# A graph layer whose issuing queue loads x before xn, and whose ScalarE takes the first norms before the tail of the previous step

## The reference, cut to what matters

```python
xn = layernorm(x)
# gnn: neighbour sum, then two linear layers
support = (1 + eps) * xn + segment_sum(edge_weight[:, None] * xn[src], dst, 12500)
gnn = relu(support @ W1.T + b1) @ W2.T + b2
# mix: 1x1 convolutions (only the centre taps meet data), hyperbolic maps, per-node linear attention
h = relu(batchnorm(conv(logmap0(proj(xn)), w_qkv)))
t = logmap0(proj(proj(expmap0(h)))); s = grouped_conv(t, w_dw, w_pw)
q, k, v = split(logmap0(proj(expmap0(concat(t, s)))))
out = attention(relu(q), relu(k), v) / (sum(v) + 1e-15)
mix = proj(expmap0(conv(logmap0(proj(expmap0(out))), w_res) + b_res))
x2 = x + gnn + mix
# ffn: one top-k over all nodes (k = 6249) picks the rows that get the FFN
x3 = layernorm(x2); w = x3 @ wr + br
y = gelu(x3 @ w1 + b1) @ w2 + b2       # kept only for the selected nodes, scaled by w
return x2 + x3 + scatter(y * w, top_k(w))
```

## Time and profile before

| | |
|---|---|
| median of 3 runs | 2587.64 us (2585.16 to 2588.34) |
| profiled execution | 2587.11 us, span of its instructions 2584.8 us |
| mean granted TensorE clock | 0.981 |
| busy share: PE, PEld, DVE, ACT, POOL | 93%, 69%, 67%, 55%, 64% |
| instructions | 44369 |

### The profile page before, as it was taken

One profiled execution on the slowest core, in us unless ns is written; L12 is line 12 of the kernel. 1 busy time (PEld: TensorE's weight loads), 2 busy tenths in 40 slices (PEclk: granted clock), 3 DMA queues, 4 the chain that ended last, 5 costly groups with the idle time before them and its releaser, 6 DMA issues.

```text
span 2584.8 us, 44369 instructions
## 1 busy us (share of the span) xinstructions
PE 2406.0 (93%) x13536; PEld 1795.6 (69%) x13536; DVE 1740.2 (67%) x5895; ACT 1431.4 (55%) x3219; POOL 1662.4 (64%) x1834
## 2 busy tenths in 40 slices
PE   4688999999999999999999999999899999999896
PEld 4665677776777776777776677777677777666686
DVE  7857576576665767657667676676766766767557
ACT  3545565565655656556555565565655656556431
POOL 1236777677776777777767777676776776777500
PEclk9889999999999999999999999999999999999998
DMA  6733444434444344443443444434444343344338
GB/s 208 252 103 103 131 116 116 117 114 131 115 118 116 113 117 123 122 121 114 116 117 114 131 115 116 118 112 125 115 122 119 114 124 110 114 132 116 88 118 283
DMA packets 225215, 327.42 MB, mean 127 GB/s; under 512 B 80845, under 2 KB 168510, under 8 KB 224956
## 3 DMA queue, kind: packets, MB, share of 16 engines
q0 software_dynamic: 84656, 231.94, 30.9%
q1 hardware_dynamic: 140300, 92.36, 12.1%
HBM read 285.70 MB, written 38.45 MB: 125 GB/s over the span
## 4 chain that ended last, share of the span: by engine, by line
PE 57%; DVE 37%; DMA 3%; issue 2%; ACT 1%; POOL 0%; SPq 0%; DVEq 0%
PE qkv L1451 14%; PE bank L1463 13%; PE bank L1356 11%; DVE rings L1155 6%; PE bank L1416 3%; PE bank L1425 3%; PE bank L1400 3%; DVE bank L1175 3%; DVE work L1180 3%; DVE work L1169 3%; DVE bank L1174 2%; PE qkv L1380 2%; DVE bank L1168 2%; DVE bank L1179 2%; DVE work L1178 2%
## 5 line engine op out<-in xcount | busy, mean ns | idle before, releaser
L958 POOL DMA_INDIRECT rings<-xn_dram,window x1715 | 1634.6, 953 | 694.3 <-issue 398.4
L1356 PE MATMUL bank<-rings 128*64 128x256 f32 x4410 | 662.7, 393 | 10.1 <-DMA rings<-xn_dram,window 7.1
L1155 DVE TENSOR_SCALAR rings<-iota,window_dst,window 128x64 f32<-128x64 f32 (+1 forms) x1715 | 490.1, 341 | 216.6 <-PE bank L1356 205.6
L1356 PEld LDWEIGHTS bank<-rings 128*64 128x64 f32 x4410 | 319.1, 137 | 276.2 <-issue 105.5
L1451 PE MATMUL qkv<-work,ffn_weights 128*128 128x256 f32 x1568 | 369.7, 384 | 0.0
L1463 PE MATMUL bank<-ffn_weights,work 128*128 128x256 f32 x1568 | 359.5, 382 | 0.0
L1463 PEld LDWEIGHTS bank<-ffn_weights,work 128*128 128x128 f32 x1568 | 293.8, 190 | 54.0 <-issue 16.2
L1048 ACT ACTIVATE work<-qkv,fb 128x256 f32<-128x256 f32 x392 | 160.1, 473 | 305.0 <-PE qkv L1451 304.5
L1451 PEld LDWEIGHTS qkv<-work,ffn_weights 128*128 128x128 f32 x1568 | 292.1, 191 | 52.5 <-ACT work L1048 16.2
L1370 PE MATMUL bank<-resident,weights 128*128 128x256 f32 x1176 | 285.6, 386 | 0.3
L1370 PEld LDWEIGHTS bank<-resident,weights 128*128 128x128 f32 x1176 | 217.7, 192 | 45.3 <-ACT work L1061 19.2
(11 more groups left out here) (261 smaller groups left out, 3267.2 us busy)
## 6 DMA issues: line engine op xcount, KB each, us to landing
rings<-xn_dram,window POOLq DMA_INDIRECT x1715
xn_dram<-work SPq DMA_DIRECT2D x14, 896.0 KB, 7.9
work<-xn_dram SPq DMA_DIRECT2D x49, 256.0 KB, 3.0
work<-in_x SPq DMA_DIRECT2D x48, 256.0 KB
out<-work SPq DMA_DIRECT2D x48, 256.0 KB
work<-in_x SPq DMA_DIRECT2D x7, 896.0 KB, 5.9
rings<-in_x SPq DMA_DIRECT2D x6, 896.0 KB, 10.0
rings<-out SPq DMA_DIRECT2D x6, 896.0 KB, 9.1
```

Source lines behind the costliest of these rows:

```text
L958: nc.gpsimd.indirect_dma_start(out=msg[G_ % RING][:, :], out_offset=None, in_=xn_dram[:, :], in_offset=bass.IndirectOffsetOnAxis(ap=window ...
L1155: v.tensor_scalar(one_hot(i, k, 0, len(quarters)), iota[:, quarters[0] * H:(quarters[-1] + 1) * H], window_dst[b][:, k:k + 1], window[b][: ...
L1356: te.matmul(agg[h][side * H:(side + 1) * H], one_hot(i, k, REACHES[k].index(q), 1), msg[gathered % RING], start=first, stop=n == STEP_PROD ...
```

## The change

Two orders are edited; no instruction is added or taken out. On SP, x of pair i - 1 is loaded before xn of pair i. On ACT, `mix_norms(i, 0)` and `mix_s_seed(i, 0)` move to the head of the step, ahead of `mix_n4_seed(j)`, `tail_supT(j)`, `ffn_x3T(m)` and `mix_exp(j)`; `tail_g1(j)` stays behind those.

```diff
@@ main_sync
             for i in range(1, NS):
+                load_x(sp, i - 1)
                 load_xn(sp, i)
-                load_x(sp, i - 1)
                 if i + 1 < NS:
                     load_window(sp, i + 1)
                 store_rows(sp, i - 1)
@@ main_scalar, step(i, j, m)
                 last = i == NS - 1
+                mix_norms(i, 0)
+                mix_s_seed(i, 0, mix)
                 if j >= 0:
                     mix_n4_seed(j, tail)
                     tail_supT(j)
                     if m is not None:
                         ffn_x3T(m)
                     mix_exp(j)
-                mix_norms(i, 0)
-                mix_s_seed(i, 0, mix)
-                if j >= 0:
                     tail_g1(j)
                 mix_v(i, 0, mix)
                 mix_norms(i, 1)
```

## The result

The changed kernel takes 2654.11 us (median of 4 runs, 2651.07 to 2656.48) against 2587.62 before: a ratio of 1.0258, 95% interval 1.024 to 1.0276, so 66 us or 2.6% slower. It is close to the time of rival 1 (2651); whether its mechanism is the one had to be tried.

The account below looks back on a forecast made before the run. PE was taken as the bound (57% of the chain), DVE carrying it where PE waits. 41 x 2.29 = 93.9 us, less 1.7, is 92.2; on 2587.1 that gives 2679 us, range 2645 to 2706.

Parts of the forecast that it names:

- rival 1: Only the late copy of the sums counts, the later `mix_v` being absorbed: 2651 us, chance 0.14.
- Part 1: On SP, x loaded before xn: DVE's wait for x goes, 1.7 us gained in all.
- the 41 steps: Steps that follow a step with an FFN; each was forecast 2.29 us longer, 93.9 in all.
- the seven other steps: The first two steps and those behind an FFN-free step; forecast to gain 7 x 0.24 = 1.7 us.
- The seed, the copy and the exponential fall behind `mix_qkv(i, 0)`: On ACT at the step's head, they wait for PE: seed done at 1062.40 instead of 1051.92, copy starts 1062.40 instead of 1059.67.
- `tail_w1` +1.61: On PE, `tail_w1` waits for the late copy and starts 1.61 us later, w2 and `combine` with it.
- `mix_v` +2.86: On ACT, the first half's `mix_v` starts 2.86 us later, because DVE's chain queues behind its wait for the seed.
- `mix_qkv(i, 1)` has no slack: On PE, it already waits for `mix_v`, so it takes over the whole 2.86 us.
- 0.57 given back by the end of the step: From the first `mix_outT` to the second half, lateness falls from 2.86 to 2.29 us, 0.50 from PE's wait at L1400.
- the first road: The late copy delays `tail_w1`, w2 and `combine`; forecast at 1.61 us a step.
- the second: The late seed delays DVE's chain, `mix_v` and `mix_qkv(i, 1)`, part given back at `mix_ft`; forecast 2.86, then 2.29 us.
- Rival 3: New PE stalls also cost it its 2.4 GHz clock, 66 us on top: 2745 us, chance 0.06.

Follow-up runs that it names:

- copy first: Changed kernel, but ACT copies the turned sums ahead of the norms, the seed staying behind them (an unread output also moves): 2765.15 us, 1.0695 of the kernel before.
- five copies: Kernel before, plus five unread ACT copies ahead of the first half's `mix_v`: 2722.54 us, ratio 1.0529.
- two copies: Kernel before, plus two unread ACT copies ahead of the first `mix_v`: 2597.26 us, ratio 1.0043.
- scale first: Changed kernel, but DVE does the first half's `mix_scale` at position 0, ahead of its wait for the seed: 2645.06 us, 1.0228 of the kernel before.
- seed-first kernel: Changed kernel, but ACT makes the n4 seed ahead of the norms again, the copy staying behind them: 2610.7 us, 1.0095 of the kernel before.

## Why the prediction was right, and where it was off

- *Part 1 gives nothing in the 41 steps, since the exponential is late next.* Shown: alone it is 1.0002. The 1.7 us that I gave the seven other steps were not there either.
- *The seed, the copy and the exponential fall behind `mix_qkv(i, 0)`.* Shown, at the places named: DVE's wait for the seed is 7.74 us (forecast 7.9), PE stalls at `tail_w1` and at `mix_qkv(i, 1)`. The latter two are 1.33 and 0.92, and not both over 1 as I wrote.
- *`tail_w1` +1.61.* Measured +1.39. I let ACT's short operations follow each other without overlap, but L1030 starts 0.11 after L1016, which itself takes 0.20, and L1010 likewise 0.11 after L981. These two make up 0.18 of the 0.22.
- *`mix_v` +2.86.* **This term was mis-sized**: +2.41. Two thirds of the miss is the time from `mix_f` to the scale. I took 2.56 for it out of the earlier trace rows; it is 2.26 after (1133.77 to 1136.03). The rows in which the step that I read (first) differs from one of the changed kernel (second):

```profile
1061.23 0.30 DVE L1205 RECIPROCAL work<-work 128x2 f32<-128x2 f32 x1
...
1062.19 0.68 DVE L1133 TENSOR_TENSOR resident<-bank,fb_row 128x512 f32<-128x512 f32 x1
1062.88 0.16 DVE L475 TENSOR_TENSOR work<-work 128x1 f32<-128x1 f32 x1
```

```profile
1134.05 0.16 DVE L1204 RECIPROCAL work<-work 128x2 f32<-128x2 f32 x1
...
1134.86 0.68 DVE L1132 TENSOR_TENSOR resident<-bank,fb_row 128x512 f32<-128x512 f32 x1
1135.46 0.15 DVE L475 TENSOR_TENSOR work<-work 128x1 f32<-128x1 f32 x1
```

Of the 0.30, 0.09 is a wait that the change removes: the scale's Newton step (L475) also needs ACT's L981, which ended at 1062.84, and so started 0.69 and not 0.60 behind the operation before it. The rest is two operations that took longer in that one step, 0.15 of it the reciprocal. In most steps of the kernel before it is the wait that counts: the stretch takes 2.50 there (median), 0.22 of it the wait for L981, which no bracket marks. The remaining 0.15 of the miss is ACT's overlap, for 0.10, and DVE's own operations between the seed and `mix_f`, for 0.05.

- *`mix_qkv(i, 1)` has no slack.* Shown: `mix_v` moved by 2.41 and it by 2.39. But PE did not yet wait there before the change, against what I wrote: in the earlier trace rows L1379 follows without a bracket. It came to the place just when ACT had freed it.
- *0.57 given back by the end of the step.* Measured 0.72, at the place named. I read the gain from PE's idle of 0.50 at L1400, and in the step read the forecast was good: first L1390 to L1400 fell there from 2.17 to 1.59. But that step, the second behind an FFN-free one, is not typical. Its length is 47.27; in most others the idle is 0.63, the distance 2.30 and the step 47.43, so that 0.71 comes back. My sentence that the steps repeat it to within some hundredths of a microsecond was wrong.
- *The sum.* The misses at `mix_v` (0.45) and at what is given back (0.15) are all but 0.02 of the 2.29 - 1.67 = 0.62 us by which a step was overestimated. In the spans the forecast was 27.0 us too long (92.2 against 65.2): 24.6 in the 41 steps (93.9 against 59.1 + 10.2), 3.4 ahead of the steps and behind them, less 1.0 in the seven others.
- *Rival 1* had the number (2651) and not the mechanism. With the copy on time and the seed late the loss is larger, not gone, and `mix_v`'s delay alone gives +1.71 a step. That 41 x 1.61, the forecast of the first road, is near 41 x 1.67, the size of the second, is chance.
- *The range.* My bounds came to 2632 and 2704, but the range stated was 2645 to 2706; the working does not show where 2645 is from. The time lies in both.
- *Rival 3*, the clock, did not happen in this kernel (0.982 against 0.981, and full clock in all 35 steps). The experiments show that it was nearer than I thought: the same lateness in one stall of 2.36 us cost clock in three steps of four. That it did not here goes with the split into two shorter stalls (1.33 and 0.92) with 7 us of products between them; I have not varied the split alone.

One rule holds the times of the steps with an FFN that lost no clock: a step grows by the larger of what the first road is late at `combine` and what the second is late at `mix_qkv(i, 1)` less 0.72. The 0.72 is taken from the changed kernel (1.67), so the others are the test. The rule gives 2.59, 1.71, 0.23 and 1.39 where 2.59, 1.71, 0.23 and 1.38 were measured (copy first, five copies, two copies, scale first), and 0.43 for the seed-first kernel, whose shorter steps have about 0.4 and whose longer ones 0.75, which the rule does not explain.

The weight load at `tail_w1` stood idle for 1.78 us until the copy was done, and started together with the first product (1132.44), as the row of before had said. The Trainium skill, page "TensorE: Matmul & The Clock Gate", section "Step-by-step: what each phase is for", says that PE can pull a weight load ahead of products still in flight. That is not the case met here: PE's products had ended when it stood, and in the kernel its wait for the copy stands ahead of the load and of the product.

## What to carry to other kernels

ScalarE was idle for 8 us a step, and yet its order mattered: what it did ahead of that idle time (the seed) was early for free. Before an engine's order is changed, look for instructions that now run early and ask what they will stand behind. When a duration between two lines is taken from a trace to be moved elsewhere, check whether each operation in it began right after the one before or on another engine's signal, and compare the step with several others: the one read here was 0.16 us shorter than most. And where two late roads meet, look from the place where they join backwards: in this kernel they did not add up, the later one counted, less the slack at the join.

## What the runs showed of the hardware that was not expected

The same stall of TensorE, 2.36 us in the same place of the same kernel, was followed by the granted clock of 1.00 in nine steps, and in 26 by a lower one, 0.51 to 0.58 over the 3.8 us of the one shown. Stalls of 3.03 us (copy first) were followed by a lower clock in 34 of 35 steps. Stalls of 0.88 us (two copies), and of 1.33 and 0.92 us (changed kernel), lowered it in none of the 35, and its mean stayed at 0.979 and 0.982. What decides between the two outcomes of the 2.36 us stall stays open.
